# Four graph layers on one core: the fourth convolution's weights turned by DMA transposes of 16-bit halves

## The reference

```python
def sage(h, Wl, Wr, b):                       # mean over the incoming edges
    return segment_mean(h[src], dst) @ Wl + b + h @ Wr
h = relu(layernorm(x)); x = x + relu(sage(h, L0_W_l.T, L0_W_r.T, b))                 # convolution 0
h = relu(layernorm(x)); h = relu(sage(h, L1_W1l, L1_W1r, b1))                        # convolution 1
x = x + sage(h, L1_W2l, L1_W2r, b2)                                                  # convolution 2
h = relu(layernorm(x))                                                               # convolution 3
neigh = segment_sum(h[dst] @ W_neigh.T + b_neigh, src) / degree
x = x + layernorm(h + relu(h @ W_self.T + b_self + neigh)) * gamma + beta
h = relu(layernorm(x)); x = x + gcn(relu(gcn(h, W1, b1)), W2, b2)                    # convolutions 4 and 5
```

## Time and profile before

| | |
|---|---|
| median of 3 runs | 650.31 us (650.18 to 650.49) |
| profiled execution | 649.73 us, span 647.9 us |
| TensorE (PE) busy | 632.0 us, 98% |
| VectorE (DVE) busy | 373.8 us, 58% |
| ScalarE (ACT) busy | 304.1 us, 47% |
| GpSimd (POOL) busy | 112.5 us, 17% |
| granted TensorE clock | 1.000 |

### The profile page before, as it was taken

How to read it: one execution, slowest core, us unless ns; L and a number is a source line. 1 busy time by engine, 2 the same in 40 slices (tenths; PEclk the granted TensorE clock), 3 DMA queues, 4 the chain that set the end, 5 groups by cost and what they waited for, 6 DMA issues and landing times.

```text
span 647.9 us, 10703 instructions
## 1 busy us (share of the span) xinstructions
PE 632.0 (98%) x3079; PEld 514.0 (79%) x3080; DVE 373.8 (58%) x863; ACT 304.1 (47%) x628; POOL 112.5 (17%) x104
## 2 busy tenths in 40 slices
PE   6989999999999999999999999999999999999997
PEld 4346777777888888888888888888888998899886
DVE  6998999766885333222333787444989730541222
ACT  4886886645334454321223342223678752555210
POOL 2000000000332300321410321430364070000000
PEclk9999999999999999999999999999999999999999
DMA  6311111228450202240201231211200000000102
GB/s 217 114 21 22 31 30 30 42 55 243 122 140 16 49 0 82 61 101 17 49 0 42 57 102 28 45 20 50 82 0 1 2 2 1 0 2 0 50 18 95
DMA packets 57953, 33.04 MB, mean 51 GB/s; under 512 B 45756, under 2 KB 49652, under 8 KB 57912
## 3 DMA queue, kind: packets, MB, share of 16 engines
q1 hardware_dynamic: 56632, 29.99, 18.0%
q10 hardware_dynamic: 1280, 2.56, 1.1%
HBM read 17.20 MB, written 4.20 MB: 33 GB/s over the span
## 4 chain that ended last, share of the span: by engine, by line
PE 91%; DVE 3%; issue 2%; DVEq 1%; DMA 1%; ACT 1%; ACTq 1%; SPq 0%
PE ps L1605 34%; PE ps L1698 27%; PE ps L1737 13%; PE ps L1763 8%; PE ps L1584 7%; DVE src_hot L1119 1%; DMA wstage<-in_L_gnn_W_l 1%; PE ps L1598 1%; PE ps L1546 1%; DVE p_lo L1373 0%; DVE stats L1091 0%; DVEq L1119 0%; DVE dst_hot L1117 0%; DVE own L1333 0%; ACTq L374 0%
## 5 line engine op out<-in xcount | busy, mean ns | idle before, releaser
L1698 PE MATMUL ps<-p_hi,cstage 128*128 128x512 f32 x400 | 156.0, 390 | 0.5 <-ACT cstage L750 0.5
L1698 PE MATMUL ps<-p_lo,cstage 128*128 128x512 f32 x400 | 155.7, 389 | 0.0
L1605 PE MATMUL ps<-w_hi,hT_hi 128*128 128x512 f32 x320 | 126.2, 394 | 0.5 <-issue 0.5
L1605 PE MATMUL ps<-w_hi,hT_lo 128*128 128x512 f32 x320 | 124.6, 389 | 0.0
L1605 PE MATMUL ps<-w_lo,hT_hi 128*128 128x512 f32 x320 | 124.6, 389 | 0.0
L1698 PEld LDWEIGHTS ps<-p_hi,cstage 128*128 128x128 f32 x400 | 75.1, 188 | 16.7 <-issue 0.9
L1698 PEld LDWEIGHTS ps<-p_lo,cstage 128*128 128x128 f32 x400 | 75.1, 188 | 15.5
L1119 DVE TENSOR_SCALAR src_hot<-iota,nodeT 128x640 bf16<-128x640 f16 x210 | 71.0, 381 | 4.0 <-issue 1.7
L1584 PE MATMUL ps<-src_hot,dst_hot 128*128 128x320 bf16 x420 | 67.5, 306 | 5.2 <-DVE src_hot L1119 2.7
L548 POOL COPY halves<-own 128x1024 uint16<-128x1024 uint16 x30 | 33.4, 1113 | 222.2 <-DVE own L1132 191.9
L1605 PEld LDWEIGHTS ps<-w_hi,hT_hi 128*128 128x128 f32 x320 | 60.1, 188 | 13.4 <-issue 1.0
(11 more groups left out here) (156 smaller groups left out, 932.9 us busy)
## 6 DMA issues: line engine op xcount, KB each, us to landing
x<-in_x ACTq DMA_DIRECT2D x1, 2304.0 KB
out_x<-x SPq DMA_DIRECT2D x9, 256.0 KB
wstage<-in_L_gnn_W SPq DMA_DIRECT2D x2, 1024.0 KB, 5.4
swap<-count SPq DMA_DIRECT2D x2, 800.0 KB, 8.6
count<-swap SPq DMA_DIRECT2D x2, 800.0 KB, 8.2
wstage<-in_L_gnn_W_l SPq DMA_DIRECT2D x2, 512.0 KB, 4.1
w_own<-in_L_gnn_W_r SPq DMA_DIRECT2D x1, 1024.0 KB, 11.0
vec<-in_L_gnn_b SPq DMA_DIRECT2D x4, 256.0 KB, 4.8
```

The source lines that it names most:

```text
L1605: last = nc.tensor.matmul(ps[:, bank, :], a[:, r, k, :], w[:, slot, k, :], start=n == 0, stop=n == len(pairs) - 1)
L1698: last = nc.tensor.matmul(ps[:, AGG + r, :], cstage[:, part, k, :], p_[:, k, :], start=n == 1, stop=n == 2 * len(parts) * NT)
```

## The change

The two matrices of the fourth convolution go through the rings of the features. Each row block of a matrix, 128 output features by 512 inputs, is treated as a tile: parted by GpSimd from `wstage`, turned by a DMA transpose, joined into `zT`, and split from there into the columns of `w_hi` and `w_lo` that belong to it. The eight blocks are numbered j = 0 to 7, 0 to 3 of the neighbours' matrix, 4 to 7 of the own one. They stand between tile 9 of L1B and tile 0 of L2 in the count of the rings (`nth_weight`; `nth` of L2 grows by 8). Parts 0 to 5 and joins 0 to 5 are ahead of GpSimd's branch, 6 and 7 inside it. ScalarE splits blocks 0 to 3 before `receive(0)`, 4 and 5 after `receive(0)`, 6 and 7 after `receive(1)`, and VectorE likewise. SyncE loads the second matrix after part 3, and its eight transposes stand ahead of those of L2. TensorE's `turn_weights` goes, and the aggregation's loop over tiles 0 to 7 is one loop again. All of the diff but context, the removed `turn_bank` and the inner lines of `turn_weights`:

```diff
@@ helpers @@
+    turned_first = [n for n, w in enumerate(weights) if w[0] == L2][0]
...
-        return NT * (s - L1A) + i + 1
+        return NT * (s - L1A) + 2 * KF * (s == L2) + i + 1
+    def nth_weight(j):
+        return NT * (L2 - L1A) + j + 1
@@ SyncE @@
-            order += loads[5:6] + turns[L2][:2] + loads[6:7] + turns[L2][2:]
+            turned_weights = [("h", (None, j)) for j in range(2 * KF)]
+            order += turned_weights[:KF] + loads[5:6] + turned_weights[KF:] + turns[L2][:2] + loads[6:7] + turns[L2][2:]
...
-                    if (s, i) == (L1A, 0):
+                    n = nth(s, i) if s is not None else nth_weight(i)
+                    if n == 1:
...
-                    sp.wait_ge(parted, nth(s, i))
-                    if nth(s, i) > 2:
-                        sp.wait_ge(joined, nth(s, i) - 2)
+                    sp.wait_ge(parted, n)
+                    if n > 2:
+                        sp.wait_ge(joined, n - 2)
...
-                    sp.wait_ge(wlo_done, KF * what)
+                    if weights[what - 1][0] == L2:
+                        sp.wait_ge(parted, nth_weight(KF * (weights[what - 1][1] + 1) - 1))
+                    else:
+                        sp.wait_ge(wlo_done, KF * what)
@@ GpSimd @@
-                    pool.wait_ge(lo_done, tile(s, i - 2))
+                    if s == L2 and i < 2:
+                        pool.wait_ge(wlo_done, KF * turned_first + 2 * KF - 1 + i)
+                    else:
+                        pool.wait_ge(lo_done, tile(s, i - 2))
...
+                def halve_weight(j):
+                    wait_loaded(pool, turned_first + j // KF)
+                    pool.wait_ge(turned_in[j % 2], 8 * (nth_weight(j - j % 2) - 1))
+                    nc.gpsimd.tensor_copy(halves[:, j % 2, :, :],
+                                          wstage[:, j % KF, :].bitcast(U16).rearrange("p (f h) -> p h f", h=2)
+                                          ).then_inc(parted, 1)
+                def join_weight(j):
+                    r = j % 2
+                    pool.wait_ge(turned_in[r], 8 * (nth_weight(j - r) + 1))
+                    if j < 2:
+                        pool.wait_ge(lo_done, tile(L1B, NT - 2 + j))
+                    else:
+                        pool.wait_ge(wlo_done, KF * turned_first + j - 1)
+                    nc.gpsimd.tensor_copy(
+                        zT[:, r, :, :].rearrange("p k n -> p (k n)").bitcast(U16).rearrange("p (f h) -> p h f", h=2),
+                        halvesT[:, r, :, :, :].rearrange("p h k n -> p h (k n)")).then_inc(joined, 1)
+                def last_weights():
+                    if s == L1B:
+                        halve_weight(6)
+                        halve_weight(7)
+                        join_weight(6)
+                        join_weight(7)
...
+                if s == L1B:
+                    for j in range(6):
+                        if j == KF:
+                            join_weight(2)
+                            join_weight(3)
+                        halve_weight(j)
+                        if j in (1, 3, 5):
+                            for k in {1: (0,), 3: (1,), 5: (4, 5)}[j]:
+                                join_weight(k)
...
-                        with pool.Fori(0, 5) as i:
+                        with pool.Fori(0, 2) as i:
+                            general_columns(i)
+                        last_weights()
+                        with pool.Fori(2, 5) as i:
...
+                        last_weights()
@@ ScalarE @@
-                    _, _, _, turned, nth = weights[n]
...
-                    if not turned:
-                        wait_loaded(act, n)
+                    wait_loaded(act, n)
...
-                        if turned:
-                            act.wait_ge(wT_ready, KF * nth + c + 1)
-                        nc.scalar.copy(w_hi[:, slot, c, :],
-                                       ps[:, turn_bank(KF * slot + c), :] if turned else wstage[:, c, :]
-                                       ).then_inc(whi_done, 1)
+                        nc.scalar.copy(w_hi[:, slot, c, :], wstage[:, c, :]).then_inc(whi_done, 1)
+            def turned_hi(j):
+                slot, k = j // KF, j % KF
+                act.wait_ge(joined, nth_weight(j))
+                mm_done(act, L1B, NT - 1)
+                nc.scalar.copy(w_hi[:, slot, :, k * P:(k + 1) * P], zT[:, j % 2, :, :]).then_inc(whi_done, 1)
...
-                    split_weights(s + 1, 0)
+                    if s + 1 == L2:
+                        for j in range(KF):
+                            turned_hi(j)
+                    else:
+                        split_weights(s + 1, 0)
...
-                    split_weights(s + 1, 1)
+                        if s + 1 == L2 and i < 2:
+                            turned_hi(KF + 2 * i)
+                            turned_hi(KF + 2 * i + 1)
+                    if s + 1 != L2:
+                        split_weights(s + 1, 1)
@@ VectorE @@
-                                                ps[:, turn_bank(KF * slot + c), :] if weights[n][3] else wstage[:, c, :],
-                                                w_hi[:, slot, c, :].bitcast(F32), ALU.subtract).then_inc(wlo_done, 1)
+                                                wstage[:, c, :], w_hi[:, slot, c, :].bitcast(F32),
+                                                ALU.subtract).then_inc(wlo_done, 1)
+            def turned_lo(j):
+                slot, k = j // KF, j % KF
+                dve.wait_ge(whi_done, KF * turned_first + j + 1)
+                nc.vector.tensor_tensor(w_lo[:, slot, :, k * P:(k + 1) * P], zT[:, j % 2, :, :],
+                                        w_hi[:, slot, :, k * P:(k + 1) * P].bitcast(F32),
+                                        ALU.subtract).then_inc(wlo_done, 1)
...
-                    split_weights(s + 1, 0)
+                    if s + 1 == L2:
+                        for j in range(KF):
+                            turned_lo(j)
+                    else:
+                        split_weights(s + 1, 0)
...
-                    split_weights(s + 1, 1)
+                        if s + 1 == L2 and i < 2:
+                            turned_lo(KF + 2 * i)
+                            turned_lo(KF + 2 * i + 1)
+                    if s + 1 != L2:
+                        split_weights(s + 1, 1)
@@ TensorE @@
-            def turn_weights(s, slot):
-                for n in weights_of(s, slot):
...
-                        for o in range(KF):
-                            last = nc.tensor.transpose(ps[:, turn_bank(KF * slot + c), o * P:(o + 1) * P],
-                                                       wstage[:, o, c * P:(c + 1) * P], ident[:, :])
-                        last.then_inc(wT_ready, 1)
...
-                        for slot, tiles in ((0, (0, 3, 2)), (1, (4, NT - 3, 2))):
-                            turn_weights(s + 1, slot)
-                            with pe.Fori(*tiles) as i0:
-                                for r in range(2):
-                                    aggregate(i0 + r, r, parts(r))
+                        with pe.Fori(0, NT - 3, 2) as i0:
+                            for r in range(2):
+                                aggregate(i0 + r, r, parts(r))
```

More of the change, by code:

```diff
@@ L255, in mm_done @@
         engine.wait_ge(q_ready if CONVS[s]["own"] else p_ready, tile(s, i))
-    def turn_bank(c):
-        return (HT, HT + 1, PP, QQ)[c] if c < KF else PP + c - KF
     def first_bank(c):
@@ L1526, in _ @@
             last.then_inc(table_pe, 1)
-            def turn_weights(s, slot):
-                for n in weights_of(s, slot):
-                    if not weights[n][3]:
-                        continue
-                    wait_loaded(pe, n)
-                    if slot == 0:
-                        pe.wait_ge(lo_done, tile(s - 1, NT - 1))
-                    else:
-                        pe.wait_ge(q_done, tile(s - 1, NT - 1))
-                        pe.wait_ge(wlo_done, KF * n)
-                    for c in range(KF):
-                        if slot == 0 and c > 1:
-                            pe.wait_ge((plo_done, q_done)[c - 2], tile(s - 1, NT - 2))
-                        for o in range(KF):
-                            last = nc.tensor.transpose(ps[:, turn_bank(KF * slot + c), o * P:(o + 1) * P],
-                                                       wstage[:, o, c * P:(c + 1) * P], ident[:, :])
-                        last.then_inc(wT_ready, 1)
             def turn_first(n, chunks):
```

## The result

| | before | after |
|---|---|---|
| median (18 runs each, same chip) | 650.16 us | 651.73 us |
| ratio, 95% interval | | 1.0028 [1.0019, 1.0036] |
| profiled execution, span | 649.73, 647.9 us | 651.93, 650.1 us |
| mean granted TensorE clock of the profiled execution | 1.000 | 0.997 |

The change makes the kernel slower by 0.28%, 1.8 us by the ratio (1.2 to 2.3) and 1.6 by the medians; the interval excludes "no change". The time is inside the range of 648.3 to 652.9 and 1.2 us above the 650.5 forecast. It lies just above the band of 649.0 to 651.6 that had the largest chance: the forecast was "the same", and what came is a little slower.

The account below looks back on a forecast made before the run. TensorE's own work was taken to bound the kernel, its feeders having a deadline each 4.54 us. Transposes -3.5, stalls +0.8 and +2.8 gave +0.1, rounded to +0.2: from the 650.31 median to 650.5 us, range 648.3 to 652.9.

Parts of the forecast that it names:

- The 3.50 us of transposes: TensorE, third convolution's aggregation: two blocks of 16 weight transposes, all on the path, are removed, -3.50 us.
- The stall before tile 3: Third convolution's aggregation: TensorE waits for VectorE's late receive of tile 1, +0.8 us.
- the one before tile 4: Third convolution's aggregation: TensorE waits for VectorE's late receive of tile 2, +2.8 us.
- the working with blocking: Chain behind the last product: VectorE and GpSimd exclude each other for whole operations; stalls of 0.8 and 2.8 us.
- the unblocked bound: Same chain if no operation blocked another: one stall of 1.5 us before tile 4, none before.
- GpSimd's jump: GpSimd's branch between join 5 and part 6: at most 1.2 us would show beside a running join; taken as 0.
- I charge nothing for the clock after a stall of 3 us: TensorE behind the stalls: granted clock assumed to stay full, 1.00, so 0 us added.
- The 0.2 by which I had rounded up: Sum of +0.1 us rounded up to +0.2 for omitted waits of 0.05 each along the chain.
- (a): Rival: chain nearly free of blocking, stall of 1.5 to 2.2 us, 648.3 to 649.0 us; chance 0.18.
- (b): Rival: GpSimd's jump delays part 6; 651.7 us with 1.2 us, 652.3 or 653.0 in worse cases; chance 0.31.
- (c): Rival: turned blocks ready in time, all 3.5 us come back, 646.8 us; needs joins 4 to 7 before 362; chance 0.05.
- (d): Rival: DMA legs of parts 4 and 6 each 1 us slower, stall 5.6 us, 652.5 us; chance 0.04.

Follow-up runs that it names:

- the control: The kernel after plus one value-neutral masking operation where tile counts are unpacked: 651.57 us, 1.0021 to the kernel before; run again 652.28 us, 1.0026.
- the second filler: Against the control, TensorE does four products into an unused bank before tile 3's aggregation and eleven before tile 4's: 652.51 us, 1.0026 to the kernel before.

## Why the prediction was right in its chain and too low in its sum

**The terms of the sum.** The 3.50 us of transposes came back as said. The stall before tile 3 was 1.14 for 0.8, the one before tile 4 2.71 for 2.8, both ended by VectorE's receive; no third stall, and ScalarE's counts weren't late. So the working with blocking held, and the unblocked bound (one stall of 1.5) is excluded: the chain, counted from the products' end, had join 4 at 9.24 for 8.95, the receive of tile 1 done at 14.67 for 14.4, that of tile 2 at 22.21 for 21.75. The legs were 3.3 for 3.1, the transfers in them 3.2 for 3.0. GpSimd's jump cost nothing, as taken: the pair of joins from 357.87 ends at 360.70, and part 6 begins at 360.62. I said some remainders would take 1 to 1.5; all four of blocks 4 to 7 took 1.25 to 1.30.

**The step that failed** is the sentence "I charge nothing for the clock after a stall of 3 us". It rested on the granted clock of 1.00 from 146 to 149.4, and in that stretch TensorE was idle for 0.55 of 3.4 us: it was no row of a stall of that length. Behind the stall of 2.7 us the clock fell to 0.51 in after and to 0.53 in the control's second profile, and took 1.5 us; in the control's first it stayed at 1.00. The Trainium skill, "TensorE: Matmul & The Clock Gate", section "HAM oscillation — how this bites in real kernels", has TensorE's clock halved behind a wait, so that the next work starts slow; the 0.51 in after agrees with that, and the 1.00 in the control's first profile doesn't. With the whole price beside my sum I would have had 652, and "slower" as the likeliest; with the 0.6 to 0.9 us that the times bear out on average, some 651.3.

**A smaller term left out** is the restart: some 0.3 us in which the first products behind each wait are slower than 0.227, twice. In the profiled execution, of the 2.48 us of the ledger my sum had +0.1; 0.25 more came by the stalls' sizes (3.85 for 3.6), 0.6 by the restarts and 1.54 by the clock. The 0.2 by which I had rounded up covers some of the first two.

**The rivals.** (a), an almost unblocked chain, is what the kernel with the remainder from PSUM shows, not this one. (b) forecast the right time, 651.7, for a wrong reason, which is luck: the jump cost nothing. It held 0.31 for another cause than the one that made the kernel slower. (c), all 3.5 us back, I held impossible short of joins before 362. The kernel with one block a tile has them all back with no join earlier, since a tile's receive stands behind one block at most. What (c) asks for holds for the order of the change, which I had taken as given, not for every order. (d) didn't occur in after; in the second filler a leg of 4.3 us put off the start of tile 4 by 1.2 us.

## What to carry to other kernels

Work that is moved from a saturated engine to its feeders must be laid out against that engine's deadlines: one block a tile (0.68 us a remainder, no stall) cost nothing, the same blocks in pairs, each a tile or more earlier and blocked, cost 3.9 us of stalls. Look for what stands ahead of the instruction that frees a buffer, and count operations that share VectorE's and GpSimd's access to SBUF at their blocked length, here 1.3 for 0.69. When TensorE gets a stall of some 2.7 us, price what comes behind it too: 0.3 us for the restart, and up to 1.5 us for the clock, which came in two of three profiles.

## What the runs showed of the hardware that I had not expected

- Behind a stall of 1.14 and then one of 2.71 us, with 4.8 us of full work between them, the granted clock was 0.51 for about 3.5 us of work; the same stalls in another execution of the same schedule left it at 1.00. With 8.5 us of idle time it fell already within the stall, and the mean clock was low in all four executions.
- The first product behind a wait takes longer at the full clock too: tile 3 took 4.83 us and not 4.54.
- DMA transposes of 128 x 1024 halves landed after 3.2 us, and after 4.3 in a stretch with an instruction load.
